# A recommendation tower in fp32: the relu of an outer round split around the copies, the squares one slot later, and 22 instead of 20 of 256 product blocks on GpSimd

## The reference, cut to what matters

```python
def _L0_rec_ref(x, Ws, bs):            # x: (B, 16, 256)
    xk = x
    outs = []
    for i in range(n_layers):          # 3
        z = jnp.einsum('bfe,bge->bfge', x, xk).reshape(B_, F_ * F_, E_)
        z = jnp.swapaxes(z, 1, 2)
        z = jnp.einsum('bcl,oc->bol', z, Ws[i]) + bs[i][None, :, None]
        z = jax.nn.relu(z)
        z = jnp.sum(z, axis=-1)
        outs.append(z)
        xk = jnp.broadcast_to(z[:, :, None], (B_, F_, E_))
    return jnp.concatenate(outs, axis=1)
...
h = jnp.concatenate([z, dense_ctx], axis=1)
h = jnp.maximum(h @ W_top1 + b_top1, 0.0)     # 64 -> 512
h = jnp.maximum(h @ W_top2 + b_top2, 0.0)     # 512 -> 256
y = h @ W_top3                                # 256 -> 1
```

## Time and profile before

| | us |
|---|---|
| median of 3 runs | 572.27 (572.27 to 573.78) |
| profiled execution, its own time | 569.55 |
| its span (first to last instruction) | 567.6 |
| busy: PE, DVE, POOL, ACT | 533.4, 524.3, 458.4, 408.5 |
| share of the span | 94%, 92%, 81%, 72% |
| granted TensorE clock | 1.000 (2.4 GHz) throughout |

### The profile page before, as it was taken

The page is one execution under the profiler, slowest core; times in us unless marked ns, Lnnn a source line. Parts: engine busy times, 40 slices in busy tenths (PEclk is TensorE's granted clock), DMA queues, the critical chain, the costliest instruction groups (busy, mean ns, idle before and its releaser), DMA issues.

```text
span 567.6 us, 17941 instructions
## 1 busy us (share of the span) xinstructions
PE 533.4 (94%) x7520; PEld 302.9 (53%) x7520; DVE 524.3 (92%) x257; ACT 408.5 (72%) x1219; POOL 458.4 (81%) x547
## 2 busy tenths in 40 slices
PE   2776999999999999999999999999999999999997
PEld 1433454555556555554655555555555555555466
DVE  4899899999999999999999999999999999999853
ACT  3566775868878686786868778786877868687743
POOL 6898999998989889897898979888897988988100
PEclk9999999999999999999999999999999999999999
DMA  3622323232232323223232322323222232322000
GB/s 89 176 69 73 86 68 89 65 93 63 64 84 68 85 59 92 60 67 86 58 94 58 83 70 65 83 63 91 61 71 79 61 86 66 86 59 71 14 2 2
DMA packets 27969, 40.57 MB, mean 71 GB/s; under 512 B 16880, under 2 KB 17264, under 8 KB 27888
## 3 DMA queue, kind: packets, MB, share of 16 engines
q0 software_dynamic: 12288, 33.57, 20.8%
q1 hardware_dynamic: 15600, 5.86, 4.2%
HBM read 38.75 MB, written 0.66 MB: 69 GB/s over the span
## 4 chain that ended last, share of the span: by engine, by line
ACT 32%; PE 28%; DVE 17%; issue 14%; POOL 6%; DMA 2%; SPq 0%; ACTq 0%; DVEq 0%; POOLq 0%
ACT relu_k L528 13%; PE sum_ps L675 12%; DVE prods L232 11%; ACT relu L517 6%; DVE relu_k L389 5%; PE outer_ps L774 5%; ACT prods L507 4%; POOL emb L285 4%; PE turn_ps L653 3%; ACT emb_t L489 3%; ACT h L559 2%; PE sum_ps L690 2%; ACT own L521 2%; POOL prods L298 1%; PE outer_ps L743 1%
## 5 line engine op out<-in xcount | busy, mean ns | idle before, releaser
L232 DVE TENSOR_TENSOR prods<-turn_ps,emb_t 128x3248 f32<-128x3248 f32 (+2 forms) x126 | 447.9, 3572 | 11.9 <-ACT emb_t L490 11.8
L285 POOL DMA_INDIRECT emb<-tables,rows_sb x256 | 252.0, 984 | 44.2 <-issue 38.0
L675 PE MATMUL sum_ps<-prods,w_sb 128*32 128x272 f32 x4096 | 264.8, 397 | 3.0 <-POOL prods L232 2.7
L675 PEld LDWEIGHTS sum_ps<-prods,w_sb 128*32 128x32 f32 x4096 | 121.3, 110 | 100.0 <-issue 13.3
L517 ACT ACTIVATE relu<-sum_ps,bias_twice 128x120 f32<-128x120 f32 x256 | 92.8, 378 | 96.5 <-PE sum_ps L675 96.4
L298 POOL TENSOR_TENSOR prods<-emb_t 128x256 f32<-128x256 f32 x128 | 95.2, 744 | 29.2 <-ACT emb_t L490 27.2
L489 ACT COPY emb_t<-turn_ps 128x512 f32<-128x512 f32 (+1 forms) x126 | 76.4, 606 | 36.5 <-PE turn_ps L653 36.4
L653 PEld LDWEIGHTS turn_ps<-ident_sb,emb 128*128 128x128 f32 x502 | 53.0, 141 | 74.2 <-DVE prods L232 53.3
L653 PE MATMUL turn_ps<-ident_sb,emb 128*128 128x128 f32 x502 | 83.2, 288 | 9.6 <-DVE prods L232 7.8
L232 POOL TENSOR_TENSOR prods<-emb_t 128x224 f32<-128x224 f32 (+1 forms) x128 | 89.9, 703 | 2.3
L528 ACT ACTIVATE relu_k<-outer_ps,bias_k 128x2048 f32<-128x2048 f32 x44 | 88.3, 2006 | 0.3 <-PE outer_ps L743 0.3
(11 more groups left out here) (81 smaller groups left out, 249.4 us busy)
## 6 DMA issues: line engine op xcount, KB each, us to landing
emb<-tables,rows_sb POOLq DMA_INDIRECT x256, 2.8
z_wide<-z_spread SPq DMA_DIRECT2D x15, 256.0 KB, 2.7
z_spread<-z_cat SPq DMA_DIRECT2D x60, 2.0 KB, 1.7
w_sb<-w_top SPq DMA_DIRECT2D x1, 512.0 KB
z_spread<-z_wide SPq DMA_DIRECT2D x2, 256.0 KB
w_sb<-w_top SPq DMA_DIRECT2D x1, 256.0 KB
ids_sb<-ids_t SPq DMA_DIRECT2D x1, 129.0 KB, 2.0
z_cat<-dense_b SPq DMA_DIRECT2D x1, 128.0 KB
```

The lines of the kernel that those rows point to most:

```text
L232: eng.tensor_tensor(out, every, shifted, ALU.mult).then_inc(done, 1)
L285: nc.gpsimd.indirect_dma_start(out=emb[:, k % EMB_RING, t * E:(t + 1) * E], out_offset=None, in_=tables, in_offset=bass.IndirectOffsetOnAx ...
L675: last = nc.tensor.matmul(sum_ps[s * 2 * F:(s + 1) * 2 * F, k % 2, 0:SUM_COLS], w_sb[:, c, odd, :], x[:, c, 2 * s + odd, :, :], start=c == ...
```

## The change

The relu of a round on ACT becomes two instructions of 1024 columns (banks 0 and 1, then banks 2 and 3). The first stands where the whole one stood, the second behind the copies of the slot. PE's rounds q=1 wait for the two halves apart, and write banks 0, 1, 2, 3 in this order for k=0 too. `fold` waits for the first half of the last round ahead of its first 32 matmuls and for the second ahead of the others (k=0). `squares` runs for tile s+1 instead of tile s+2, behind the copies and ahead of `relu_pairs`. POOL takes 3 blocks in six slots of 8 instead of four, and DVE two blocks fewer a group. `outer_relu` counts two to a round.

```diff
-POOL_THREE = (0, 2, 4, 6)
+POOL_THREE = (0, 1, 2, 4, 5, 6)
...
-            def relu_round(k, g, q):
+            def relu_round(k, g, q, half):
...
-                nc.scalar.activation(relu_k[:, k, q, :, :].rearrange("p j n -> p (j n)"), outer_ps[:].rearrange("p j n -> p (j n)"),
+                j = slice(half * 2, half * 2 + 2)
+                nc.scalar.activation(relu_k[:, k, q, j, :].rearrange("p j n -> p (j n)"), outer_ps[:, j, :].rearrange("p j n -> p (j n)"),
...
-                    relu_round(*ROUND_AT[slot - 1])
+                    relu_round(*ROUND_AT[slot - 1], 0)
...
                 if slot != 1:
                     take_turned(ahead)
+                if slot - 1 in ROUND_AT and (ROUND_AT[slot - 1][0], ROUND_AT[slot - 1][2]) != (1, 1):
+                    relu_round(*ROUND_AT[slot - 1], 1)
+                if slot == 1 or slot > 2:
+                    squares(3 if slot == 1 else slot + 1)
...
                 relu_pairs(slot)
                 if slot in SIDE_AT:
                     take_side(slot, *SIDE_AT[slot])
-                if slot != 1:
-                    squares(ahead)
...
-                if q > 0:
-                    pe.wait_ge(outer_relu, ROUND_NO[k, g, q])
-                for j in ((2, 3, 0, 1), (0, 1, 2, 3))[k]:
+                for j in ((2, 3, 0, 1), (0, 1, 2, 3))[k] if q == 0 else range(J):
+                    if q > 0 and j % 2 == 0:
+                        pe.wait_ge(outer_relu, RELUS * ROUND_NO[k, g, q] - 1 + j // 2)
...
-                pe.wait_ge(outer_relu, ROUND_NO[k, g, TURNS - 1] + 1)
                 for q in range(k, TURNS):
+                    pe.wait_ge(outer_relu, RELUS * ROUND_NO[k, g, TURNS - 1] + q + 1)
                     last = add_round(k, q, outer_ps[:, FOLD_BANK[k], 0:P], q == k, q == TURNS - 1)
```

More of the change, by code:

```diff
@@ L70 @@
 ROUND_NO = {of: n for n, of in enumerate([ROUND_AT[s] for s in sorted(ROUND_AT)] + END_ROUNDS)}
+RELUS = 2
 SIDE_ORDER = sorted([(PER * g + at, what, g) for g in range(GROUPS) for what, at in
@@ L385, in relu_add @@
                 dve.wait_ge(outer_done, n + 1)
-                dve.wait_ge(outer_relu, n)
+                dve.wait_ge(outer_relu, RELUS * n)
                 at_least(dve, fold_done[1], g)
@@ L389, in relu_add @@
                 nc.vector.scalar_tensor_tensor(out=second, in0=outer_ps[:].rearrange("p j n -> p (j n)"), scalar=bias_less[:],
-                                               in1=first, op0=ALU.max, op1=ALU.add).then_inc(outer_relu, 1)
+                                               in1=first, op0=ALU.max, op1=ALU.add).then_inc(outer_relu, RELUS)
             def reduce_fields(k, g, src):
@@ L673, in sum_pairs @@
                                 if (c, odd, s) == (1, 1, 3) and (g := group_at(k, PROJ)) is not None and g > 0:
-                                    pe.wait_ge(outer_relu, ROUND_NO[1, g - 1, TURNS - 1] + 1)
+                                    pe.wait_ge(outer_relu, RELUS * (ROUND_NO[1, g - 1, TURNS - 1] + 1))
                                 last = nc.tensor.matmul(sum_ps[s * 2 * F:(s + 1) * 2 * F, k % 2, 0:SUM_COLS], w_sb[:, c, odd, :],
@@ L812, in _ @@
                 if slot == STEPS - 1:
-                    pe.wait_ge(outer_relu, ROUND_NO[0, PREV, 1] + 1)
+                    pe.wait_ge(outer_relu, RELUS * (ROUND_NO[0, PREV, 1] + 1))
                     hidden1(LAST - 2, h1_banks)
```

## The result

The changed kernel took 575.56 us (median of 7 runs), the kernel before 572.84 beside it (7 runs): ratio 1.0046, 95% interval 1.0033 to 1.0059. It is slower by more than the bound of 0.3%; 567.7 was forecast, 572.4 was the upper end of the range. The same two kernels give 0.990 in two other jobs (a job is one session of measurements on one chip, with the kernel before run beside the others); the experiments show both. I take the trace of this slower result first. Its profiled execution took 575.32 us.

What follows compares the result with a forecast made beforehand. Each group was a ring through ACT and DVE costing 0.50 us over PE's work; PE would become the bound. Span 567.6 + 0.4 - 4.8 - 0.5 + 0.4 = 563.1; 4.5 off the median gave 567.7 us, range 565.5 to 572.4.

Steps and rivals of the forecast that it cites:

- The median of the runs is 2.7 over the profiled one; I take the same 4.5 off it: Whole run: the 4.5 us saved in the profiled execution also comes off the median, giving 567.7 us.
- rival B: Slots 2 to 4: the `z_wide` transfer replaces PE's 0.21 us wait for DVE, so 570.2 us; chance 0.14.
- PE becomes the bound: Each group: PE sets the pace at 32.83 us, 0.40 less than before; chance 0.62.
- What there is to free: PE's waits for DVE at slot 4 (0.21) and for ACT ahead of the fold (0.29), together 0.50 us a group.
- Squares at nothing: ACT: squares behind the copies still end over 1 us before PE uses them at slot 6, so no cost.
- The wait for the second half in the round: Round of slot 5: PE newly waits 0.10 us a group for the second relu half.
- So the 0.29 wait goes, with 0.2 us to spare: Fold of k=0: the second half ends at 303.6, before PE needs it at 303.8, so the wait ahead goes.
- DVE reaches the product of slot 4 earlier and its wait goes: Slot 4: earlier copies bring DVE there about 1 us sooner, so PE's 0.21 us wait goes.
- `z_wide`, 0.4 us in all: Slots 2 to 4: the transfer's margin shrinks by 0.21 us; lateness shows in two of thirteen groups, 0.4 us more.
- GpSimd's blocks: Two more blocks cost POOL 0.41 us a group and save DVE 0.21; PE is 0.4 us later at slot 27.
- D: Round of slot 5: PE waits 0.6 us for a late second half, so slower, 574.3 us; chance 0.09.
- C: The 0.50 us returns as PE waiting for the second half, or DVE was no part; say 572; chance 0.15.

Runs made afterwards that it cites:

- e13: The changed kernel run again unaltered, in a job of kind B: 564.99 us, ratio 0.9898 to the kernel before.
- e11: The changed kernel without the halves (squares moved, 22 blocks for GpSimd, relu whole): 560.90 us, ratio 0.9818, kind B.
- e1: The kernel before with only the third block of slots 1 and 5 of 8 given to GpSimd: 574.73 us, ratio 1.003, kind A.
- e17: The changed kernel run again unaltered, in a job of kind A: 575.79 us, ratio 1.0044 to the kernel before.
- e18: The changed kernel with both relu halves ahead of the copies, in a job of kind A: 567.08 us, ratio 0.9894.
- e2: The kernel before with only the squares moved one slot later, behind the copies; relu whole, 20 blocks: 562.27 us, ratio 0.981, kind A.
- e5: The kernel with only the squares moved, plus a second, already fulfilled wait of PE in mid-fold: 561.05 us, ratio 0.984, kind B.
- e16: The kernel before, run once for its trace in a job of kind B: 569.87 us, no late semaphore.
- e3: The changed kernel with GpSimd back at 20 blocks: 573.27 us, ratio 1.0009 to the kernel before, kind A.
- e14: The changed kernel with both relu halves ahead of the copies, in a job of kind B: 562.63 us, ratio 0.9861.
- e15: The changed kernel with only the fold's relu whole and ahead of the copies, the others in halves: 562.52 us, ratio 0.9863, kind B.
- e9: The changed kernel run again unaltered, in an earlier job of kind B: 565.53 us, ratio 0.9899 to the kernel before.
- e8: The kernel before with squares moved and 22 blocks for GpSimd, relu whole: 560.87 us, ratio 0.9832, kind B.
- e10: The changed kernel with both relu halves ahead of the copies, in an earlier job of kind B: 562.99 us, ratio 0.9853.

## Why the prediction was wrong

**The step that failed first** is "The median of the runs is 2.7 over the profiled one; I take the same 4.5 off it". Those 2.7 us were not an offset: the trace is of kind B, the runs of before and the result of kind A. In kind B the forecast nearly holds: 4.5 off the 570.75 of e13's job is 566.3, and 564.99 was measured (ratio 0.992 forecast, 0.990 measured). Part of that is luck, for the errors of its terms cancel: PE's need is 0.23 us a group less than taken, the wait for `z_wide` 0.23 more and the round's 0.06 more (e13 against e11, and the points below). The 2.7 us don't explain the result: in kind A the change makes the kernel slower, and there two more steps fail, the fold's and that of DVE and slot 4. Set against the 32.50 us of e11, the result's period of 33.74 has 0.57 more at the fold of k=0, 0.43 at sum 4, 0.16 at round 4 and 0.10 at round 5. The prediction saw the 2.7 us, and rival B gave them to DMA.

**PE becomes the bound**: right, in both kinds (77% of the chain, and 78% in e13).

**What there is to free**: the two brackets of the earlier trace rows, 0.50 us, were too little. From start to start the fold's wait is 2.33 - 1.86 = 0.47 and the one of slot 4 is 1.26 - 0.99 = 0.27, 0.74 together, since matmul rows overlap and a bracket counts only what is left between them. PE's need is 32.50 us (e11), not the 32.73 of the earlier trace rows. In kind A more was to be freed: e1 has 1.42 and 2.51 at these two places, 1.08 over the least.

**Squares at nothing**: right. They alone give 0.981 in kind A, 10.7 us, over twice the forecast for the whole change.

**The wait for the second half in the round**, taken as 0.10: 0.16 in kind B (1.24 against 1.08), 0.07 to 0.10 in A. The sign of over 0.3 us a group at line 747 did not come.

**"So the 0.29 wait goes, with 0.2 us to spare"**: in kind B right; the half ends 0.85 after the fold's start and the fold costs 0.02 more. **In kind A this is the step of the working that failed**: what stands behind the fold starts 2.44 us after it instead of 1.90, so the 0.5 us comes back there. Shown by e17 and e18, side by side: with both halves ahead of the copies the fold is at 2.00. The lateness of the half goes with it. In e17 it ends 0.6 to 1.05 after the fold's start, in e2 before it (1.90). In e18 both occur: in eight folds from 137 us on it ends 0.25 to 0.43 after the start, and the first and the last matmul of seven of them start 1.66 to 1.73 apart (one 1.99); in three it ends 0.78 to 0.80 after, and these start 1.97 to 2.00 apart, in one 0.60 and 1.79. Lateness alone doesn't give the size: in e17 folds with the half 0.85 behind have 2.24 to 2.27 where e18 has 2.00 at 0.8, and e17's first fold (at 72.84) has 1.66 with the half 0.60 behind. A fulfilled wait costs nothing in kind B (e5; not run in A). Why the loads stop in the second half of the fold, behind a wait that is over by then, is not shown.

**DVE reaches the product of slot 4 earlier and its wait goes**: right there, but in kind A the changed kernel's signal at the end of the fold of k=1 comes 0.9 us late and DVE's reduce waits for it (14.4 us in 15 times over the whole trace, 2.8 in 2 in e16), so PE waits at slot 5 instead: round 4 is 1.24 to 1.33. In sum, e3 against e2: the fold's 0.54, this 0.25 and the round's 0.07, less 0.08 at sum 6, are 0.8 us a group, 9.4 in twelve, of the 11.0 between them.

**`z_wide`, 0.4 us in all**: much too little. Sum 4 is 0.31 longer in e13 than in e16, 3.7 us over twelve groups, which is rival B's mechanism and more than its price of 0.21. In kind B it is not there with the relu whole (2.05 in e11), with both halves ahead (2.07 in e14), nor where only the fold's relu is whole (2.03 in e15, which keeps the other halves around the copies). In kind A sum 4 is 2.25 in e2 without any halves, and 2.48 in the result. ACT's copy of z0 starts 3.19 us after PE's matmul for it in e9, e11 and e16 alike; what differs is the time from SP's first issue of `z_spread` to that of `z_wide`, 3.89 us in e9 and 3.45 in e11 on the mean of twelve groups. It doesn't explain it alone, for it is 3.77 in e16, where PE comes to sum 4 later by its wait, and 3.7 in e13. Whether the gathers stand in its way is not shown.

**GpSimd's blocks**: in kind B nothing in either direction (e8 beside e5). In kind A about 2 us (e1; the result against e3), where sum 4 grows from 2.26 to 2.48; the start of 0.4 explains a part only.

**The rivals**: D had the right sign, a time near the measured one (574.3) and the wrong place, so that is luck: the round of slot 5 waits 0.1, not 0.6. C (the 0.50 comes back as waiting for a late second half) is the nearest for kind A, at the fold and not at the round. The rule of the Trainium skill on the price of an ACTIVATE ("ScalarE: Activation LUTs", "Rules for kernel authors") did not decide: a half costs 304.75 - 303.75 = 1.00 us from start to start, as in the earlier trace rows, and the halves ahead cost 562.99 - 560.90 = 2.1 us against the whole relu (e10, e11).

**Open**: what makes a job kind A or B. Chip 3 gave A, chips 12 and 6 gave B, and chip 5 gave B and then A, so the chip alone doesn't settle it. What a trace of the kernel before looks like in kind A is open too. Why the signal of the fold of k=1 is mostly later with the halves (0.6 to 1.0) than in e2 (up to 0.38) isn't settled either.

The best version is neither kernel: the squares moved, 22 blocks, the relu whole, 0.982 to 0.983 in kind B (not run in A); the squares alone take 0.981 in A.

## What to carry to other kernels

When the profiled execution is faster than all plain runs of the same kernel, its trace may be of another condition than the runs: compare PE's semaphore times with its rows before reading slack of under a microsecond from it. A half that is ready only while its consumer already runs was hidden in one kind of job here and cost 0.5 us in the other; both halves ahead of the copies, or the producer whole, was faster in both. Try the cheapest part of a change (here the squares) alone first, and measure a small gain in more than one job.

## What the runs showed of the hardware

- The same program has two conditions, and which holds is a matter of the job: 572.8 to 573.2 and 570.2 to 570.8 us for the kernel before, ratios of the changed kernel of 1.0044 and 1.0046 against 0.9899 and 0.9898. The granted clock is 0.996 to 1.0 in both, but for one of the fast executions (0.95, the kernel before in job 3).
- In kind A a PE semaphore comes up to 1.05 us after the end that its matmul row shows: in e2 1.03 at the fold of k=0, 0.5 at the transposes behind it, 0.2 at the next sum. It is late at folds, transposes and sums, never by 0.1 us at the long matmuls of the outer rounds (at most 0.07). In e2 the rows behind the fold start 1.88 us after it all the same, as in kind B. The Trainium skill, "Perfetto Trace Analysis", "Summary: the profiler window per engine type", has TensorE's end as an estimate that leaves the semaphore out. The traces agree: in kind B the two differ by 0.01 to 0.06 us at all but four places (up to 0.13), in kind A by up to 1.05.
- A wait of PE that is fulfilled before PE reaches it costs nothing (e5, kind B); where the wait in the middle of 64 short matmuls was fulfilled 0.6 to 0.85 us after the first, the next bundle started about 0.54 us later in kind A (e3 against e2) and 0.02 later in kind B (e13 against e11).
- Halves of 1024 columns on ACT follow each other 1.00 us apart, and a whole relu of 2048 takes 1.85, so a cut cost ACT 0.15 us here.
